# Three edits in a hybrid attention, FFN and state-space kernel: how routing weights are spread over partitions, the order of one LoRA block, and the order of output parts in attention

## The reference

```python
x = x + attn_a(layernorm(x), wq, wk, wv, wo)     # 16 heads, 4 KV heads, head size 128,
                                                 # each query sees 4 first keys and the last 32
x = x + ffn(layernorm(x), ...)
x = x + attn_b(layernorm(x), ...)                # state-space mixer
x = x + ffn(layernorm(x), ...)

def ffn(x):                                      # 8 experts, 2 per token, LoRA rank 16, hidden 704
    topw, sel = top_k(x @ gate_w.T, 2)
    topw = softmax(topw, axis=1)                 # over the 1024 TOKENS, for each of the two slots
    for e in range(8):
        c = sum(where(sel == e, topw, 0))        # this token's weight for expert e
        up   = x @ w_up.T   + 2 * (x @ up_A[e].T   @ up_B[e].T)
        gate = x @ w_gate.T + 2 * (x @ gate_A[e].T @ gate_B[e].T)
        ch = c[:, None] * silu(up) * gate
        mixed += ch
        lora  += 2 * (ch @ down_A[e].T @ down_B[e].T)
    return mixed @ w_down.T + lora
```

## Time and profile before

| what | value |
|---|---|
| median of 3 runs | 557.07 us |
| the profiled execution, and its span | 557.08 us, 555.3 us |
| TensorE busy | 523.4 us (94%) |
| VectorE busy | 402.6 us (73%) |
| ScalarE busy | 310.6 us (56%) |
| GpSimd busy | 126.9 us (23%) |
| granted TensorE clock, mean | 0.996 |
| attention, about | 0 to 214 us |
| first FFN, about | 214 to 341 us |
| mixer, about | 341 to 432 us |
| second FFN, about | 432 to 555 us |

### The profile page before, as it was taken

How to read it: one execution, slowest core, us unless ns; L and a number is a source line. 1 busy time by engine, 2 the same in 40 slices (tenths; PEclk the granted TensorE clock), 3 DMA queues, 4 the chain that set the end, 5 groups by cost and what they waited for, 6 DMA issues and landing times. The chain is left out here.

```text
span 555.3 us, 9124 instructions
## 1 busy us (share of the span) xinstructions
PE 523.4 (94%) x3049; PEld 441.6 (80%) x3049; DVE 402.6 (73%) x897; ACT 310.6 (56%) x768; POOL 126.9 (23%) x272
## 2 busy tenths in 40 slices
PE   5998899999999979999989999999998999999996
PEld 4777799999998967688878888757777778878885
DVE  5534465665665878799787899866886677878767
ACT  3655877688687643474343455988662254333332
POOL 2332434344243310000000003569433000000000
PEclk9999999999999999999999999999999999999999
DMA  7320000000002103000030000000000000000101
GB/s 267 112 78 1 18 22 2 1 1 2 2 2 102 47 1 138 1 1 1 5 129 0 2 0 1 1 1 2 1 0 2 0 1 1 1 1 0 39 1 38
DMA packets 5790, 14.25 MB, mean 26 GB/s; under 512 B 624, under 2 KB 2928, under 8 KB 5744
## 3 DMA queue, kind: packets, MB, share of 16 engines
q1 hardware_dynamic: 5744, 13.66, 6.9%
HBM read 12.61 MB, written 1.05 MB: 25 GB/s over the span
## 5 line engine op out<-in xcount | busy, mean ns | idle before, releaser
L167 PE MATMUL psum<-xT_hl,ffn_w_hl 128*128 128x512 f32 x312 | 77.8, 397 | 3.1 <-DVE f_t L1232 3.1
L167 PE MATMUL psum<-f_um,ffn_w_hl 128*128 128x512 f32 x288 | 72.6, 399 | 1.4 <-DVE f_t L1232 1.3
L167 PEld LDWEIGHTS psum<-xT_hl,ffn_w_hl 128*128 128x128 f32 x312 | 56.3, 188 | 15.0 <-issue 4.0
L167 PEld LDWEIGHTS psum<-f_um,ffn_w_hl 128*128 128x128 f32 x288 | 53.2, 188 | 14.8 <-DVE f_um L1244 3.1
L1129 ACT ACTIVATE f_sil<-psum 128x512 f32<-128x512 f32 (+1 forms) x48 | 28.6, 596 | 63.1 <-PE psum L167 62.8
L1232 DVE TENSOR_TENSOR f_t<-psum,f_sil 128x512 f32<-128x512 f32 (+1 forms) x48 | 33.2, 691 | 30.0 <-ACT f_sil L1129 29.3
L691 DVE TENSOR_TENSOR pT_hl<-psum,pT_hl 126x360 fp32r<-126x360 f32 (+1 forms) x44 | 23.6, 537 | 42.9 <-ACT pT_hl L598 42.9
L167 PE MATMUL psum<-wo_hl,oT_hl 128*128 128x256 f32 x384 | 50.8, 282 | 4.0 <-DVE oT_hl L697 4.0
L167 PE MATMUL psum<-xT_hl,wq_hl 128*128 128x512 f32 x192 | 52.3, 407 | 1.9 <-ACT qT L566 1.9
L167 PEld LDWEIGHTS psum<-wo_hl,oT_hl 128*128 128x128 f32 x384 | 47.7, 188 | 7.5 <-DVE oT_hl L697 5.9
L566 ACT ACTIVATE qT<-psum 128x512 f32<-128x512 f32 x32 | 34.9, 1091 | 31.6 <-PE psum L167 31.6
(11 more groups left out here) (238 smaller groups left out, 1130.4 us busy)
## 6 DMA issues: line engine op xcount, KB each, us to landing
w_raw<-in_wq SPq DMA_DIRECT2D x4, 512.0 KB, 4.1
w_raw<-in_wo SPq DMA_DIRECT2D x4, 512.0 KB, 3.2
ffn_w_raw<-in_ffn SPq DMA_DIRECT2D x3, 576.0 KB, 5.7
ffn_w_raw_far<-in_ffn SPq DMA_DIRECT2D x3, 576.0 KB, 5.0
ssd_w_raw<-in_ssd SPq DMA_DIRECT2D x3, 512.0 KB, 5.0
x_resid<-in_x SPq DMA_DIRECT2D x2, 512.0 KB, 4.4
out_x<-x_resid SPq DMA_DIRECT2D x4, 256.0 KB, 2.2
w_raw<-in_wk SPq DMA_DIRECT2D x1, 512.0 KB, 6.3
```

Of the source, the lines that this page charges most:

```text
L167: i = e.matmul(dst, lhs(a), rhs(b), start=start and n == 0, stop=stop and n == len(TERMS) - 1, **kw)
```

## The change

It has three parts.

**1. Routing weights.** VectorE writes the 16 weight columns eight times side by side (`w_rep`, 128x128). TensorE transposes that in one go. ScalarE copies the result as the high part (`wr`), and VectorE makes rows 32 to 63 of it the low part and keeps rows 0 to 31 as the high part, by one operation with a column of the parameters (CS_LO). Then the rows are multiplied with a column that keeps the rows of one tile only, once for each tile: for the first half on ScalarE (`wr0`), for the second on GpSimd (`wr1`). `slot_rows` holds, for each slot, ones in that slot's rows. One float32r matmul of 512 columns for each slot and half then gives what four float32 matmuls gave. On VectorE parts 6 and 7 of `masked(0)` come behind `gated(0, 0)`, and `second(0)` waits in two steps, for part 5 and then for part 7.

**2. Block 6.** TensorE issues `base_lora(6)` ahead of `second(5)` as in all other turns. On VectorE `masked(1)` parts 2 and 3 come together in turn 5, and parts 4 to 7 together at the start of turn 6.

**3. Attention.** `oT_lo` comes ahead of `add` in a step, and `norm0` too. At the start, ScalarE takes the exponentials behind the value block's high part, the first unit's in two pairs; and the eighth product of queries (`Q_PAIR`) goes to bank 7, so that it needn't wait for bank 6.

```diff
-            RECIPS = {NJ - 5: 0, NJ - 3: 1}
+            RECIPS = {NJ - 4: 0, NJ - 2: 1}
+            EXPS = {NJ - 6: (0, (0, 1)), NJ - 5: (0, (2, 3)), NJ - 4: (1, range(NB_Q)), NJ - 2: (2, range(NB_Q))}
+            Q_PAIR = 2 * GROUP - 1
...
-                    if n:
+                    if n and n != Q_PAIR:
                         e.wait_ge(s_qt, n)
                     for k in range(KB):
-                        m = three(e, bank(6), lambda w: wq_hl[:, g % 2, w, k, h * HD:(h + 1) * HD],
+                        m = three(e, bank(7 if n == Q_PAIR else 6), lambda w: wq_hl[:, g % 2, w, k, h * HD:(h + 1) * HD],
...
+                def exps(u, some=None):
                     e.wait_ge(s_max, u + 1)
                     if u >= 4:
                         e.wait_ge(s_rd, u - 3)
                     rows, parts, p = probs(u)
-                    for n in range(parts):
+                    for n in range(parts) if some is None else some:
                         m = e.activation(p[:, n, :], p[:, n, :], ACT.Exp, bias=NEGM[0:rows, u % 4, n:n + 1],
                                          accum_out=DEN[0:rows, u % 4, n:n + 1])
-                    m.then_inc(s_exp, 1)
+                    if n == parts - 1:
+                        m.then_inc(s_exp, 1)
 
                 w_hi(e, 3)
                 w_hi(e, 4)
                 for j in range(NJ):
-                    if j in FIRST_UNITS:
-                        exps(FIRST_UNITS[j])
                     e.wait_ge(s_v, j + 1)
                     e.activation(v_hl[0:NK[j], HI, j, :], bank(4 + j % 2)[0:NK[j], :], ACT.Copy).then_inc(s_vhi, 1)
                     if j < GROUP:
                         q_evac(j)
+                    if j in EXPS:
+                        exps(*EXPS[j])
...
+                    if 0 <= i - LAG_F < NU:
+                        oT_lo(i - LAG_F)
+                    if i == NU + 1:
+                        early(phase, "norm0", e)
                     if i in y_tile:
                         add(y_tile[i])
                         if y_tile[i] >= (KV - 1) * NT:
                             early(phase, "stats", e, y_tile[i] % NT)
-                    if 0 <= i - LAG_F < NU:
-                        oT_lo(i - LAG_F)
-                    for step, stage in ((NU, "veps0"), (NU + 1, "norm0"), (NU + 2, "lo0"), (NU + 3, "logits_copy0"),
-                                        (NU + 4, "split0")):
+                    for step, stage in ((NU, "veps0"), (NU + 2, "lo0"), (NU + 3, "logits_copy0"), (NU + 4, "split0")):
...
-                        need(e, "um", 8 * h + 8)
+                        need(e, "um", 8 * h + 6)
                     need(e, "t0", i + 1)
                     for which in range(2):
+                        if b == 0 and which:
+                            need(e, "um", 8 * h + 8)
                         m = three(e, to_bank(i, which), lambda w: blk(w, b, (FB_UPB, FB_GTB)[which]),
                                   lambda w: um_hl[:, h, 1, which, w, :], False, True, skip_group_check=True)
                     m.then_inc(FS["b"], 1)
 
                 def weigh(h):
-                    need(e, "wt", 1)
+                    need(e, ("wr0", "wr1")[h], 1)
                     if h:
                         need(e, "wbc", 2)
                     for s in range(SLOTS):
-                        for i in range(HT):
-                            t = HT * h + i
-                            m = e.matmul(bank(wb_bank(h, s))[:, i * P:(i + 1) * P],
-                                         WT[:, s, t:t + 1].broadcast_to([P, P]), ident, start=True, stop=True)
-                        m.then_inc(FS["wb"], 1)
+                        e.matmul(bank(wb_bank(h, s)), slot_rows[:, s, :], wr_rhs[:, h].rearrange("p t n -> p (t n)"),
+                                 start=True, stop=True).then_inc(FS["wb"], 1)
...
                 base_lora(e, 0)
+                need(e, "top_dve", TOP_DVE["wt"])
+                e.transpose(bank(7)[:, 2 * P:3 * P], w_rep, ident).then_inc(FS["top_pe"], 1)
                 base_lora(e, 1)
                 second(0)
...
-                        if i == MASK_STEP + 2:
-                            second(i - 1)
                         base_lora(e, i)
                     if i == N:
                         early(phase, "tr0", e)
-                    if 2 <= i <= N and i != MASK_STEP + 2:
+                    if 2 <= i <= N:
...
+                for n in range(SLOTS):
+                    e.activation(slot_rows[:, n, :], ones, ACT.Copy, scale=par[:, WR_SLOT + n:WR_SLOT + n + 1])
...
+                need(e, "top_pe", TOP_PE["wT"])
+                e.activation(wr, bank(7)[:, 2 * P:3 * P], ACT.Copy).then_inc(FS["wrh"], 1)
                 silu(0, 0)
+                need(e, "top_dve", TOP_DVE["wlo"])
+                for t in range(HT):
+                    m = e.activation(wr_rhs[:, 0, t, :], f32(wr), ACT.Copy, scale=par[:, WR_HALF + t:WR_HALF + t + 1])
+                m.then_inc(FS["wr0"], 1)
...
+                need(e, "top_pe", TOP_PE["sum"])
+                e.reciprocal(RS, bank(7)[:, P + 2:P + 4]).then_inc(FS["top_dve"], 1)
+                need(e, "top_dve", TOP_DVE["rs"])
+                copies = P // (SLOTS * NT)
+                wide = [P, copies, SLOTS, NT]
+                e.tensor_tensor(w_rep.rearrange("p (q k t) -> p q k t", q=copies, k=SLOTS),
+                                EX.rearrange("p (o k) t -> p o k t", o=1).broadcast_to(wide),
+                                RS.rearrange("p (o k u) -> p o k u", o=1, u=1).broadcast_to(wide),
+                                ALU.mult).then_inc(FS["top_dve"], 1)
+                masked(0, 4, 5)
+                need(e, "wrh", 1)
+                e.scalar_tensor_tensor(out=wr, in0=f32(wr), scalar=par[:, CS_LO:CS_LO + 1], in1=bank(7)[:, 2 * P:3 * P],
+                                       op0=ALU.mult, op1=ALU.add).then_inc(FS["top_dve"], 1)
                 gated(0, 0)
+                masked(0, 6, 7)
...
+                    if i == MASK_STEP + 2:
+                        masked(1, 4, 5, 6, 7)
                     if i < N and i != 1:
                         slot(i, 0)
                     if i == MASK_STEP + 1:
-                        masked(1, 2)
-                    if i == MASK_STEP + 2:
-                        masked(1, 4, 5)
+                        masked(1, 2, 3)
...
-                        masked(1, 3)
                         mask_diff(1)
-                    if i == MASK_STEP + 2:
-                        masked(1, 6, 7)
...
+                need(e, "top_dve", TOP_DVE["wlo"])
+                for t in range(HT):
+                    m = e.tensor_scalar(wr_rhs[:, 1, t, :], f32(wr), par[:, WR_HALF + HT + t:WR_HALF + HT + t + 1], None,
+                                        ALU.mult)
+                m.then_inc(FS["wr1"], 1)
...
+    at_tile = (k[:, None] % 32 < SLOTS * NT) * ~later * (k[:, None] % NT == np.arange(NT)[None, :])
+    at_slot = 1.0 * (k[:, None] // NT % SLOTS == np.arange(SLOTS)[None, :])
+    return np.concatenate([-1.0 * lo, at_head * ~later, at_head * later, -at_chunk * later, at_chunk * ~later, 1.0 * ~later,
+                           at_tile, at_slot], 1).astype(np.float32)
```

53 lines of the change are left out of this document (27 added, 26 removed).

## The result

The changed kernel takes 544.50 us (median of 4 executions, 543.93 to 545.39). The kernel before was run once more beside it and has 557.02 us over 4 executions (556.63 to 557.43). The ratio is 0.978, 95% interval 0.976 to 0.979. The forecast was 547.2 us: the direction and the range are right, and the gain was 2.7 us larger than the sum of 9.9. The profiled execution of the changed kernel took 545.39 us, with a span of 543.3; TensorE is busy 516.2 us (95%) instead of 523.4.

A forecast was written before the change was run, and what follows sets the result against it. TensorE was taken as the bound nearly everywhere. Attention's start 3.2, steps 1.0 and 0.2, end 1.7, routing weights 0.8 and block 6 3.0 sum to 9.9 us: 557.08 - 9.9 = 547.2 us, range 544.3 to 550.3.

The forecast's parts named there:

- Attention's start: Start of attention: waits for v_hl (1.8 us) and the eighth queries' wait for qT (1.4) go, 3.2 together.
- Attention's steps: Attention's steps: low output part no longer behind an add; 1.0 us from three waits, 0.2 from others for oT_hl.
- the part is ready 0.4 earlier: Attention's steps: low output part comes 0.4 us earlier without the add ahead, so three waits of 0.34 go, 1.0.
- rival 3: Attention: delayed adds hold bank 7 for 0.42 us longer, 32 adds cost 13.4, time 560.6 us; chance 0.03.
- The term of 0.2: Attention's steps: gain from the remaining waits for oT_hl, taken as 0.2 us, bounds 0 and 1.5.
- Attention's end: End of attention: waits of 0.80 and 1.22 go, 0.84 comes back, 0.50 from the last stretch; 1.7 us.
- Routing weights: Both FFNs' spreads: TensorE's work falls by 4.5 us, but little arrives; 0.8 together, bounds -1.0 and 4.5.
- rival 2: FFNs: the spreads' saved work does arrive, weights give 3.5 instead of 0.8, time 544.5 us; chance 0.10.
- when it did, or a little before: Routing weights: second(0) begins as before, at 451.3 or a little earlier; no gain counted.
- The contention: FFNs: GpSimd's products beside VectorE's two masked products lengthen these by 0 to 1.2 us, taken as 0.3.
- rival 4: FFNs: masked products stretch to their upper bound, block 6 loses its cover; weights -1.0, time 549.6 us; chance 0.10.
- Block 6: Both FFNs: TensorE's wait of 1.36 us for the gated product goes, 1.5 each, 3.0 together, bounds 2.4 and 3.0.

The follow-up runs named there:

- no_start: The changed kernel with only attention's start undone (exponentials ahead of the value blocks' high parts, eighth queries in bank 6): 548.04 us.
- no_att: The changed kernel with the low output part behind the add again, and the normalised tiles behind add and stats: 547.20 us.
- split_wait: The kernel before with one edit: second() of a half's first block waits for its masked products in two steps, 6 then 8 of 8: 556.37 us.
- only_weights: The kernel before with the routing weights part of the change alone: 554.54 us over 8 executions.
- twice_first: The changed kernel with each matmul of the first spread of routing weights issued twice: 545.25 us.
- no_b6: The changed kernel with only block 6's order undone, on TensorE and for VectorE's masked parts 3 to 7: 549.73 us.
- twice_second: The changed kernel with each matmul of the second spread of routing weights issued twice: 545.96 us.
- both_new: The changed kernel with the edits of pv_first and sil_first together: 542.30 us.
- gpsimd_idle: The changed kernel with GpSimd's four products for the second half moved to ScalarE: 544.49 us.
- all_three: The changed kernel with the edits of pv_first, sil_first and gpsimd_idle together: 541.82 us.
- sil_first: The changed kernel with the wait before base products split: the first six wait for the silu, the others for the gated product: 543.42 us.
- pv_first: The changed kernel with p_v ahead of the projection in attention steps where the step before projected too: 544.67 us.

## Why the prediction was right, and where it wasn't

**Attention's start: right.** 3.2 predicted, 3.4 by no_start, at the two places predicted.

**Attention's steps: the sum right, the step wrong.** The failed step is "the part is ready 0.4 earlier: 3 x 0.34 = 1.0". I looked up what the projection waits for by its bracket, which names only the last of its conditions. The code has a second one, the add in bank 7. These three waits stayed as waits for the add, 0.41 instead of 0.34. That was rival 3's mechanism, at 0.09 instead of 0.42, in three places instead of 32. The term of 0.2 with bounds 0 and 1.5 was the one that paid: waits of 0.3 to 0.5 in front of `p_v`, three of them hidden, 1.25 us by 182.57 net of the loss. That the sum of both terms, 1.2, came out is luck: two errors cancelled.

**Attention's end: right.** 1.7 predicted, 1.55 measured, and term by term. The changed kernel, TensorE and then VectorE, which answer to 204.72 of the earlier trace rows and to the earlier trace rows:

```profile
197.56 1.32 PE L237 MATMUL psum<-const_f,xn 128*128 128x128 f32 x8 [0.16 <-DVE xn L229]
...
200.31 1.65 PE L169 MATMUL psum<-wo_hl,oT_hl 128*128 128x256 f32 x12 [0.94 <-DVE oT_hl L703]
```
```profile
205.26 0.42 DVE L710 TENSOR_TENSOR x_resid<-psum,x_resid 128x256 f32<-128x256 f32 x1 [0.26 <-PE psum L169]
...
208.12 0.42 DVE L710 TENSOR_TENSOR x_resid<-psum,x_resid 128x256 f32<-128x256 f32 x1
```

and no_att's two adds:

```profile
208.30 0.42 DVE L710 TENSOR_TENSOR x_resid<-psum,x_resid 128x256 f32<-128x256 f32 x1 [0.73 <-PE psum L169]
...
211.60 0.42 DVE L710 TENSOR_TENSOR x_resid<-psum,x_resid 128x256 f32<-128x256 f32 x1
```

Against no_att the wait of 0.80 that went gives 0.96, that for the tiles, down from 1.22 to 0.16, gives 1.10, and the projection behind the transposes, which waits 0.94 for the output part, takes 0.99 back (predicted 0.84). From the sixth tile's add to the last it is 208.12 - 205.26 = 2.86 instead of 211.60 - 208.30 = 3.30, 0.44 (predicted 0.50). What I hadn't listed are longer waits for oT_hl at two projections ahead of this, 0.55 at 184.76 and 1.13 at 192.69; the steps between give as much, so by 192.69 they come to nothing. Steps and end together: 2.9 predicted, 2.8 by no_att. no_att moves `norm0` and `oT_lo` together, so the split between steps and end rests on the landmarks alone.

**Routing weights: mechanism right.** The net gains of first and second FFN were to be 0.1 and 0.7. With the 0.31 and 0.32 of split_wait taken off, only_weights leaves 0.09 and 0.76. The first spread's saving did turn into the wait for the gated product, and by twice_first that work wasn't on the path; rival 2 is out. Two things were missed. I said `second(0)` would begin "when it did, or a little before" and put the little at nothing; it was 0.27 in the first FFN and 0.30 in the second (0.40 in the wait for f_t, less the transpose). And I read the split wait in the diff for the first half only, where it is used up by the order around it; for the second half it took away 0.6 us that I hadn't priced, since the wait sat in the middle of a group of matmuls. The contention that I put at 0.3 for each FFN was 0.1; rival 4 is out. By only_weights the part is worth 2.05 where 0.8 was predicted, so this is the term of the sum that was most in error.

**Block 6: right.** 3.0 predicted, 3.3 by no_b6. The wait of 498.87 is gone, and the step before keeps its cover. The changed kernel, TensorE and VectorE, which answer to the earlier trace rows:

```profile
478.98 2.89 PE L169 MATMUL psum<-xT_hl,ffn_w_hl 128*128 128x512 f32 x12
...
487.31 1.99 PE L169 MATMUL psum<-xT_hl,ffn_w_hl 128*128 128x512 f32 x8
```
```profile
477.97 0.69 DVE L1252 TENSOR_TENSOR f_t<-psum,f_sil 128x512 f32<-128x512 f32 x1
...
482.35 2.50 DVE L1264 TENSOR_TENSOR f_um<-f_us,f_mT 128x512 fp32r<-128x512 f32 x4
...
486.20 0.70 DVE L1252 TENSOR_TENSOR f_t<-psum,f_sil 64x512 f32<-64x512 f32 x1
```

The first gated product ends 0.3 ahead of TensorE (predicted 0.2), the last 0.4 ahead (predicted 0.3).

**The sum.** By the stretches the change gives 11.3 us, and by the runs on its parts 3.4 + 2.8 + 3.3 + 2.05 = 11.6, where 9.9 were predicted: 0.6 more of the split wait, 0.6 of the earlier `second(0)`, 0.3 of block 6 and 0.2 of the start. The 0.3 between the two sums lie in attention's stretch, where before can't be compared more closely than to 0.4.

The measured 12.5 are more than that, and the rest isn't shown to be the edits' work. The low clock at the end of the mixer, 1.5 us, is in nearly all executions of before (10 of 13, 16 of 17 and 7 of 9 in the three comparisons), but in one of the four of the changed kernel. So the median of before contains it, and that of the changed kernel doesn't. Whether the change made it rarer, or chance did, stays open: of the kernels derived from it twice_first and twice_second have it in none of 5, no_start, no_att and both_new in 1, gpsimd_idle and all_three in 2, sil_first and pv_first in 3, and no_b6 in all. With it the changed kernel would take some 546.0 us, an estimate from 544.5 + 1.5 (its one execution with the low clock took 545.39).

The range of 544.3 to 550.3 held the time, by 0.2 us. The time is also, to the tenth, the 544.5 that rival 2 forecast, but by coincidence: the work of the first spreads did not arrive.

## What to carry to other kernels

- A bracket names the last releaser. Before a wait is counted as removed, read in the code every semaphore of the waiting instruction, and see when the second last one comes: it may be that of the instruction that the edit pushes behind.
- A time that fits a forecast, or a rival, proves neither. Here 544.5 was rival 2's figure, and doubling the work in question showed that it wasn't on the path.
- A reordering pays where one of two consumers needs only the one that moves ahead. Look for waits inside groups too, by the weight loads and by the distance between two groups' starts, as the matmul rows don't show them.
- Work that TensorE does just ahead of a wait for the chain that it has started is free. Saving it gives nothing; splitting that wait by bank did.

## What the runs showed of the hardware that I hadn't expected

- A stretch of some 3.4 us at the lower clock at one place of the mixer, present in some executions of a kernel and absent in others, worth 1.5 us. In the kernel before TensorE was busy 2.97 of 4 us ahead of it; in no_att it was busy 3.12 of 4 us at this place and the clock stayed at 1.00. What decides it these rows don't show.
- GpSimd beside VectorE: one masked product took 0.78 us instead of 0.68, while GpSimd's own, 0.60 us alone and 0.61 beside an instruction that reads PSUM, took 1.11 and up to 1.98 beside ones that read two SBUF tiles.
- The keys' start varies from 19.6 to 21.7 us between the 14 profiled executions; the first wait, for the constants' DMA, varies only from 5.0 to 5.5.
